# Pair sums of a mixture-of-experts layer, added by VectorE from PSUM instead of SBUF, with 24 buffers for the expert outputs instead of 16

## What is computed

```
x = x + attn(layernorm(x))
xf = layernorm(x)
weights, indices = top_k(softmax(xf @ Wg), 4)
y[token] += swiglu(xf[token], W1[e], W2[e], W3[e]) * weight   # for each of a token's four experts
z = swiglu(xf, Ws1, Ws2, Ws3)                                 # silu(xf @ Ws1) * (xf @ Ws3) @ Ws2
out = x + y + z
```

## Time and profile before

| | us |
|---|---|
| median of 3 runs | 640.11 |
| lowest and highest | 639.14, 641.84 |
| time of the profiled execution | 639.03 |
| its span | 637.3 |
| last stage, from the first h matmul at 551.39 to the end | 85.9 |
| mean granted clock of TensorE | 0.973 |

### The profile page before, as it was taken

One profiled execution on the slowest core, in us unless ns is written; L12 is line 12 of the kernel. 1 busy time (PEld: TensorE's weight loads), 2 busy tenths in 40 slices (PEclk: granted clock), 3 DMA queues, 4 the chain that ended last, 5 costly groups with the idle time before them and its releaser, 6 DMA issues.

```text
span 637.3 us, 16757 instructions
## 1 busy us (share of the span) xinstructions
PE 581.1 (91%) x4081; PEld 420.9 (66%) x4081; DVE 365.5 (57%) x1420; ACT 393.3 (62%) x1306; POOL 375.0 (59%) x425
## 2 busy tenths in 40 slices
PE   4799999999999977699899999999999999997981
PEld 1466766666676654268668888888888888554551
DVE  4589999999999995433223233322333223248686
ACT  2589988989898973216656766676666766410100
POOL 4124778787788786605445555565665555497360
PEclk9999999999999997699999999999999999998995
DMA  8994444444444547957776655565565555397773
GB/s 275 303 291 167 175 169 179 178 161 169 187 161 169 200 185 231 348 173 226 235 224 190 184 181 184 181 186 182 182 182 185 187 180 181 113 412 251 228 264 132
DMA packets 70154, 130.53 MB, mean 205 GB/s; under 512 B 10288, under 2 KB 48560, under 8 KB 70064
## 3 DMA queue, kind: packets, MB, share of 16 engines
q1 hardware_dynamic: 52128, 83.32, 41.1%
q0 software_dynamic: 13824, 41.96, 17.8%
q10 hardware_dynamic: 4112, 4.19, 2.0%
HBM read 61.11 MB, written 68.32 MB: 203 GB/s over the span
## 4 chain that ended last, share of the span: by engine, by line
PE 65%; POOL 10%; issue 8%; DVE 8%; SPq 4%; ACT 3%; DMA 2%; DVEq 0%; ACTq 0%; POOLq 0%
PE pS L730 19%; PE pS L742 9%; PE pS L554 8%; POOL xs L369 6%; PE pQV L659 4%; PE pS L590 3%; POOL w L387 3%; PE pT L723 2%; PE pO L676 2%; PE pQV L723 2%; PE pQV L568 2%; PE pO L568 2%; PE pO L642 1%; DVE xall L994 1%; PE pT L631 1%
## 5 line engine op out<-in xcount | busy, mean ns | idle before, releaser
L398 POOL DMA_INDIRECT ys<-gsh,dst x160 | 152.9, 956 | 131.9 <-ACT gsh L531 130.0
L730 PE MATMUL pS<-w,after_a 128*128 x640 | 165.8, 382 | 0.2 <-ACT after_a L520 0.2
L369 POOL DMA_INDIRECT xs<-xg,posi x128 | 124.3, 971 | 49.6 <-issue 25.6
L730 PEld LDWEIGHTS pS<-w,after_a 128*128 128x128 f32 x640 | 109.1, 190 | 9.8 <-issue 0.6
L742 PE MATMUL pS<-w,after_a 128*128 x320 | 95.6, 381 | 0.0
L1008 DVE COPY after_a<-pO 128x128 f32<-128x128 f32 x80 | 23.3, 292 | 93.0 <-PE pO L737 92.0
L1008 DVE COPY after_a<-pT 128x128 f32<-128x128 f32 x80 | 23.3, 292 | 92.8 <-PE pT L737 91.4
L531 ACT ACTIVATE gsh<-pS,xg 128x256 f32<-128x256 f32 x160 | 75.9, 474 | 0.4 <-issue 0.4
L530 ACT CAST dst<-xg 128x1 int32 x160 | 30.6, 191 | 60.9 <-PE pS L742 60.9
L659 PE MATMUL pQV<-w 128*128 128x512 f32 x128 | 64.0, 624 | 0.5 <-ACT w L464 0.5
L554 PE MATMUL pS<-x2T_all,ws 128*128 128x512 f32 x128 | 62.1, 640 | 2.4 <-DVE gsh L978 1.4
(11 more groups left out here) (157 smaller groups left out, 1105.8 us busy)
## 6 DMA issues: line engine op xcount, KB each, us to landing
xg<-xs SPq DMA_DIRECT2D x160, 160.0 KB, 2.2
ys<-gsh SPq DMA_DIRECT2D x32, 512.0 KB
w<-ys SPq DMA_DIRECT2D x32, 512.0 KB, 6.2
xs<-padrow SPq DMA_DIRECT2D x33, 160.0 KB, 2.4
w<-in_L_ffn_W ACTq DMA_DIRECT2D x1, 4096.0 KB, 21.9
out<-xall SPq DMA_DIRECT2D x32, 128.0 KB, 1.8
xall<-in_L_attn_X SPq DMA_DIRECT2D x1, 3072.0 KB, 14.0
ys<-gsh,dst POOLq DMA_INDIRECT x160, 2.7
```

What stands on the lines that cost most here:

```text
L369: pool.indirect_dma_start(out=xs, out_offset=bass.IndirectOffsetOnAxis(ap=posi[:, a.r8, k:k + 1], axis=0), in_=xr[:, a.r8, :], in_offset=N ...
L398: pool.indirect_dma_start(out=ys, out_offset=bass.IndirectOffsetOnAxis(ap=dst[:, j % 8:j % 8 + 1], axis=0), in_=y[:, j % 8, :], in_offset= ...
L730: last = pe.matmul(pS[a.b][:, 0:2 * F], xgT[:, a.b, k, :], w13[:, bass.ds(e, 1), k, :, :].rearrange("p a n f -> p (a n f)"), start=(k == 0 ...
```

## The change

- *The adds.* Behind GpSimd's sum, ScalarE copies both 128x256 sums of a tile from SBUF to a PSUM bank, `pT0` or `pT1` in turn (`copy_parts`, L552 of the new kernel). VectorE adds first the one half of the bank to `xall`, then the other (`add_parts`, L1060 and L1062), the second waiting for the first by `half_sum`. So there are two adds a tile as before, but each has one input in SBUF and one in PSUM. ScalarE fills a bank again when the tile two earlier is added (`added`).
- *The buffers.* `PB` is 24; the eight more lie where the expert weights `w2` were (`arena`).
- *SP.* It issues 24 loads, then the other 8, each when `parts_copied` says that ScalarE has copied the tile 24 earlier, and only then the 32 stores, each when its tile is complete.
- *Which addition comes last.* Up to tile 15 (`LATE` = 4 groups) z is added first and the parts last; from tile 16 on the parts come first and z last.
- *The order.* On VectorE and ScalarE it is written out step by step. TensorE's order is unchanged; its wait for z adds is split over two semaphores.

```diff
-    PB = 16
+    PB = 24
...
+        def parts(t):
+            b = t % PB
+            return parts_a[:, b] if b < 16 else parts_b[:, b - 16]
...
-            for t in range(NT + PB):
-                if t >= PB:
-                    sp.wait_ge(S["summed"], t - PB + 1)
-                    sp.dma_start(out_tiles[t - PB], xall[:, t - PB, :]).then_inc(final[t % 2], 16)
-                if t < NT:
-                    sp.dma_start(parts[:, t % PB, :, :], ys_tiles[t]).then_inc(parts_in[t % PB], 16)
+            for t in range(PB):
+                sp.dma_start(parts(t), ys_tiles[t]).then_inc(parts_in[t], 16)
+            for t in range(PB, NT):
+                sp.wait_ge(S["parts_copied"], t - PB + 1)
+                sp.dma_start(parts(t), ys_tiles[t]).then_inc(parts_in[t - PB], 16)
+            for t in range(NT):
+                if t < QT * LATE:
+                    sp.wait_ge(S["added"], t + 1)
+                else:
+                    sp.wait_ge(S["summed"], t - QT * LATE + 1)
+                sp.dma_start(out_tiles[t], xall[:, t, :]).then_inc(final[t % 2], 16)
...
-            for g in range(NPRE, NG):
-                shared_silu(g)
-
+            def copy_parts(t):
+                wait(act, S["parts_sum"], t + 1)
+                wait(act, S["added"], t - 1)
+                act.copy((pT0, pT1)[t % 2][:], parts(t)[:, 0:2, :].rearrange("p k c -> p (k c)")
+                         ).then_inc(S["parts_copied"], 1)
+
+            half_silu(2, 0)
+            half_silu(2, 1)
+            copy_parts(0)
...
-                    wait(pe, S["z_done"], QT * g + q - 1)
+                    wait(pe, S["z_done"], min(QT * g + q - 1, QT * LATE))
+                    wait(pe, S["summed"], QT * (g - LATE) + q - 1)
...
-                for t in range(g * QT, (g + 1) * QT):
-                    wait(dve, S["parts_sum"], t + 1)
-                    dve.tensor_tensor(parts[:, t % PB, 0, :], parts[:, t % PB, 0, :], parts[:, t % PB, 1, :], ALU.add
-                                      ).then_inc(S["half_sum"], 1)
-                for t in range(g * QT, (g + 1) * QT):
+            def add_parts(t):
+                wait(dve, S["parts_copied"], t + 1)
+                if t < QT * LATE:
                     wait(dve, S["z_done"], t + 1)
-                    wait(dve, S["half_sum"], t + 1)
-                    dve.tensor_tensor(xall[:, t, :], xall[:, t, :], parts[:, t % PB, 0, :], ALU.add).then_inc(S["summed"], 1)
+                dve.tensor_tensor(xall[:, t, :], xall[:, t, :], (pT0, pT1)[t % 2][:, 0:D], ALU.add).then_inc(S["half_sum"], 1)
+                wait(dve, S["half_sum"], t + 1)
+                dve.tensor_tensor(xall[:, t, :], xall[:, t, :], (pT0, pT1)[t % 2][:, D:2 * D], ALU.add).then_inc(S["added"], 1)
```

More of the change, by code:

```diff
@@ L533, in _ @@
             pipelined(NJ, 3, expert_step)
-            for g in range(NPRE, NG):
-                shared_silu(g)
+            def copy_parts(t):
[6 more added lines that the diff above has]
+            copy_parts(0)
+            copy_parts(1)
+            half_silu(3, 0)
+            copy_parts(2)
+            copy_parts(3)
+            half_silu(3, 1)
+            copy_parts(4)
+            copy_parts(5)
+            copy_parts(6)
+            copy_parts(7)
+            copy_parts(8)
+            half_silu(4, 0)
+            copy_parts(9)
+            copy_parts(10)
+            copy_parts(11)
+            half_silu(4, 1)
+            copy_parts(12)
+            copy_parts(13)
+            copy_parts(14)
+            copy_parts(15)
+            copy_parts(16)
+            half_silu(5, 0)
+            copy_parts(17)
+            copy_parts(18)
+            half_silu(5, 1)
+            copy_parts(19)
+            copy_parts(20)
+            copy_parts(21)
+            copy_parts(22)
+            copy_parts(23)
+            half_silu(6, 0)
+            copy_parts(24)
+            copy_parts(25)
+            copy_parts(26)
+            half_silu(6, 1)
+            copy_parts(27)
+            copy_parts(28)
+            copy_parts(29)
+            copy_parts(30)
+            copy_parts(31)
+            half_silu(7, 0)
+            half_silu(7, 1)
         @block.tensor
@@ L978, in shared_gate, with add_z @@
-                    dve.tensor_tensor(gsh[:, g % 2, m, :], sg[:, m, :], pS[2 * m + 1][:], ALU.mult).then_inc(S["gsh_done"], 1)
+                    half_gate(g, m)
+            def add_z(t):
+                wait(dve, S["z_ps"], t + 1)
+                if t >= QT * LATE:
+                    dve.wait_ge(S["added"], t + 1)
+                dve.tensor_tensor(xall[:, t, :], xall[:, t, :], (pQV, pO)[t % 2][:, 0:D], ALU.add
+                                  ).then_inc(S["z_done" if t < QT * LATE else "summed"], 1)
@@ L980, in shared_add @@
             def shared_add(g):
                 for q in range(QT):
[L982 to L991 removed]
+                    add_z(g * QT + q)
@@ L1016, in _ @@
                 dve.wait_ge(y_out[b], 16 * NJ // 8)
-            shared_gate(NPRE)
-            for g in range(NG):
-                if NPRE + 1 + g < NG:
-                    shared_gate(NPRE + 1 + g)
-                if NPRE + g < NG:
-                    shared_add(NPRE + g)
-                parts_add(g)
+            half_gate(2, 0)
+            half_gate(2, 1)
+            add_parts(0)
+            add_parts(1)
+            half_gate(3, 0)
+            add_parts(2)
+            add_parts(3)
+            half_gate(3, 1)
+            add_parts(4)
+            add_z(8)
+            add_z(9)
+            add_parts(5)
+            add_z(10)
+            add_z(11)
+            add_parts(6)
+            add_parts(7)
+            add_parts(8)
+            half_gate(4, 0)
+            add_parts(9)
+            add_parts(10)
+            add_parts(11)
+            half_gate(4, 1)
+            add_z(12)
+            add_z(13)
+            add_parts(12)
+            add_z(14)
+            add_z(15)
+            add_parts(13)
+            add_parts(14)
+            add_parts(15)
+            add_parts(16)
+            half_gate(5, 0)
+            add_parts(17)
+            add_parts(18)
+            half_gate(5, 1)
+            add_parts(19)
+            add_z(16)
+            add_z(17)
+            add_parts(20)
+            add_z(18)
+            add_z(19)
+            add_parts(21)
+            add_parts(22)
+            add_parts(23)
+            half_gate(6, 0)
+            add_parts(24)
+            add_parts(25)
+            add_parts(26)
+            half_gate(6, 1)
+            add_parts(27)
+            add_z(20)
+            add_z(21)
+            add_parts(28)
+            add_z(22)
+            add_z(23)
+            add_parts(29)
+            add_parts(30)
+            add_parts(31)
+            half_gate(7, 0)
+            half_gate(7, 1)
+            add_z(24)
+            add_z(25)
+            add_z(26)
+            add_z(27)
+            add_z(28)
+            add_z(29)
+            add_z(30)
+            add_z(31)
 _INS = ["L0_attn_X", "L0_attn_Wq", "L0_attn_Wv", "L0_attn_q_norm_w", "L0_attn_v_norm_w", "L0_ffn_Wg", "L0_ffn_W1",
```

26 lines of the change are left out of this document (14 added, 12 removed).

## The result

| | before | after |
|---|---|---|
| median, us | 639.71 (4 runs, 639.14 to 641.84) | 622.31 (4 runs, 620.32 to 623.50) |
| ratio | | 0.972, 95% interval 0.9686 to 0.9754 |
| profiled execution: time, span | 639.03, 637.3 | 622.96, 621.2 |
| last stage, first h matmul to the end | 637.3 - 551.39 = 85.9 | 621.2 - 552.42 = 68.8 |
| mean granted clock | 0.973 | 0.986 |

The forecast was 623.3 in a range of 620.5 to 628.5. The kernel is 17.4 us faster by the medians, and the last stage is 17.1 us shorter by the profile (it began 1.03 us later in this execution, so the spans differ by 16.1).

A forecast was written before the change was run, and what follows sets the result against it. It took the last stage as bound by 64 VectorE adds, half held by GpSimd, ahead of z adds TensorE awaits. Undisturbed span 617.9 plus 2.6 of waits is 620.5, a gain of 16.8 from 640.11: 623.3 us, range 620.5 to 628.5.

The forecast's parts named there:

- the three waits: TensorE in z(2), z(4), z(5): a pair of adds ahead of the first z add delays it 0.87 us, 2.6 together.
- the hold: Last stage: VectorE adds with both inputs in SBUF each wait out one GpSimd sum, taking 1.2 to 1.4 us.
- three of about 1.3: TensorE in z(2), z(4), z(5): idle times of about 1.3 us each, counting the 0.41 us already there.
- GpSimd's starvation: GpSimd's sums: loads ahead of all stores would feed its 32 sums without a break, the last done at 599.2.
- The term of 0.58 us a store: SP's queue: each store costs 0.58 us, so 24 stores are gone by 611 and all 32, if ready, by 615.6.
- The tail: End of the kernel: the last store costs 2.68 us between VectorE's last add and the span's end, and stays.
- A: Rival: stores behind the last load set the end, at 0.77 us each; 625 us, chance 12%.
- B: Rival: TensorE's clock falls at its three waits of 1.3 us, costing 5.1 us; 628.4 us, chance 6%.
- C: Rival: VectorE's adds from PSUM wait for GpSimd as well, so no gain; 640 us, chance 3%.
- D: Rival: tiles come too slowly, delaying the end from 1.59 us a tile on; 643 us, chance 4%.
- E: Rival: TensorE's three waits for VectorE in z(2), z(4), z(5) don't come; 620.7 us, chance 8%.
- The page's price of PSUM operands: VectorE's 64 adds: the skill page charges 0.065 us more each from PSUM, 4.1 us of VectorE time together.

The follow-up runs named there:

- e4: Kernel after, with VectorE's pair of part adds moved behind the first two z adds in groups 2, 4 and 5; 619.78 us, 0.967 of before.
- e12: Kernel after, but VectorE adds from SBUF without ScalarE's copies and GpSimd sums only 8 of 256 columns of each half; 0.974 of before.
- e11: Kernel before plus only ScalarE's copies and the adds from PSUM; 16 buffers, old SP and VectorE order; 0.986 of before.
- e1: Kernel before with only 24 buffers and all loads ahead of all stores on SP; 640.75 us, 0.999 of before.
- e3: Kernel after with 16 buffers instead of 24; 622.27 us, 0.970 of before.
- e10: Kernel after with 16 buffers and SP's old sequence, each store followed by the load of the tile 16 later; 0.975 of before.
- e6: Kernel after with a second ScalarE copy of the same size, into unused SBUF, ahead of each copy to PSUM; 626.65 us, 0.978 of before.
- e7: Kernel after with the second add of each tile taken from SBUF instead of PSUM; 0.981 of before.
- e2: Kernel after without ScalarE's copies, VectorE adding both halves straight from SBUF; 642.06 us, 1.002 of before.

## Why the prediction was right

*The sum.* Each term beside what it measured:

| term | forecast | measured |
|---|---|---|
| TensorE from h(2) to its end, with three waits | 614.81 - 551.39 + 2.6 = 66.0 | 66.15 |
| the three waits, in z(2), z(4), z(5) | 3 x 0.87 = 2.6 | 0.80 + 0.89 + 0.89 = 2.58; gone in e4, worth 2.4 |
| pair of adds, start to start | 0.80 (0.46 + 0.34) | 0.79 (567.69 to 568.48) |
| ScalarE's copy | 0.65 (0.59 to 0.95) | 0.59 |
| last z add | 0.42 | 0.45 |
| end of VectorE to the end of the span | 2.68 | 2.2 |
| stage | 69.1 | 68.8 |

The step that carried it was to build TensorE's undisturbed schedule from the chain's 10.60 us periods and to add the waits that the new order leaves. It asked of VectorE only that it be early enough, and with 42.3 us of work in the 72 us from 550 to 622 it was.

*The size of the waits.* That 2.58 was measured where 2.6 was said is in part luck. The sum let the pair wait for ScalarE's copy, 0.67 us behind the gate's start. It starts 0.60 behind it (567.09 to 567.69), and 0.61 in e12, where there is no copy: at its 0.59 us the copy is in time, and the pair costs 0.79, not 0.87. What filled the sum up is the 0.1 us of z(4) and z(5) that stays in e4. And "three of about 1.3" did not come: the 0.41 us from which it was counted is idle time of the weight loads, while the matmuls stood still for 0.17 there (566.09 to 567.13, where 0.87 is the usual step). Theirs became 0.80 to 0.89.

*What bounds the stage.* The prediction read the hold out of the earlier trace rows and named it as the bound. e12 shows the hold to be what it was taken for. But "that is what bounds the last stage" was too simple: with the hold gone and the order as before (e11), the stage is 9.8 us longer than after. The sum was right all the same, since it took the tail of parts behind the last z add as gone, which only the new order makes it. The prediction should have named the two gains apart, 8.6 us on TensorE and 8.0 behind it. Whoever had read it as "the PSUM adds are worth 17 us" would have been wrong by 10.

*The buffers and SP's order.* "This takes GpSimd's starvation away" is true and worth nothing (e1, e3, e10). "24 loads go at once" is not true: SP needs 19.3 us for them. The consequences that were drawn held nevertheless. The last sum ends at 601.5; 599.2 was said for a stage that began 1.03 earlier, so it is 1.3 later, by 1.2 us of short waits for DMA. The stores ready by then were gone at 608, with 611 forecast, as a window of the kernel after shows, the first with the DMA idle (0.06; it was 0.82 in the 2 us before):

```profile
608.00:610.00 2.00, 2.00 (x6) 0.89 (x5) 0.69 (x1) 0.52 (x1) 0.00 (x0) 1.00 0.06 18
```

The term of 0.58 us a store was too dear: SP's queue had 75.9% of 72 us, 54.6 us, which less 32 loads at 1.25 is 0.46 each.

*The tail.* It was 2.68 and is 2.2, because the last tiles now end 0.86 apart and SP has nothing else to issue: the last store is issued at 619.1, right behind the add that ends at 619.02; before, with adds 0.335 apart, it was issued at 635.0, 0.4 behind the add that ended at 634.62. This and e11's tail of 692.2 - 690.0 = 2.2 agree.

*The rivals.* A (stores set the end): no, the DMA is idle between 608 and the stores of the last tiles. B (the clock falls): no, each 2 us window from 554 to 620 has a granted clock of 1.00. But the waits were 0.8 to 0.9 us and not the 1.3 that B assumed; at 1.33 and 1.42 (e6, e7) the matmuls kept their pace too, and behind some longer waits they did not, see below. C (PSUM adds are held too): no, as the single lines of the kernel after show, that of the copy first (durations ns least/median/most):

```profile
L552 ACT COPY pT<-w x32: 587/590/592, 560.7 to 605.8; 128x512 f32<-128x512 f32 x32
```

```profile
L1060 DVE TENSOR_TENSOR xall<-xall,pT x32: 412/416/422, 561.4 to 606.4; 128x256 f32<-128x256 f32 x32
```

D (slow tiles): no, but e10 comes near its threshold of 1.59, with 1.49 us a tile. E (no waits): no, but e4 shows what it is worth: 2.5 us against the median of e3, 2.4 by the traces, where 2.6 was said.

*The page's price of PSUM operands.* The Trainium skill (VectorE: DVE Perf Modes, the section on the TRN2 errata) would have made each add 0.065 us dearer than one from SBUF, an estimate from its cycle counts. e12 has the comparison that was missing, the same add from an SBUF that nobody holds: 0.418 us (L1057) against 0.416 from PSUM (L1060), and 0.424 against 0.421 for the second add of a pair. The rows decide: in this kernel they cost the same.

## What to carry to other kernels

An engine that is slowed by a neighbour (here VectorE's adds with both inputs in SBUF beside GpSimd's) costs twice: what waits for it, and the work that is then still left behind the last step. Removing the slowdown gives the first only; the second needs an order that uses the freed time, and that order alone can make things worse while the slowdown is there, so both have to be tried together. Before buffers are added to feed an engine, look whether anyone waits for it, and whether the issuing queue could fill them; and in front of an add that TensorE waits for, put nothing that can stand behind it.

## What the runs showed of the hardware that was not expected

- SP's issue of DMAs gets slower while many are in flight: 24 loads of 512 KB took 19.3 us to issue, where 16 took 8.94 in the kernel before; single issues took up to 2.98 us, and the later loads landed 15.7 to 17.1 us after their issue. So a load can wait at SP although its buffer is free.
- The hold costs both sides: GpSimd's sums take 1.38 us each beside SBUF adds (e2) and 1.28 beside PSUM adds.
- TensorE's clock: behind waits of 1.33 and 1.42 us (e6, e7) the z tiles kept their 1.03 to 1.13 us; behind waits of 1.87 (e1), 1.98 (e6) and 2.65 us (e7) some ran slower, 1.52 to 1.91 us a tile, and the ten us from there on have a granted clock of 0.83 in each (597 to 607, 604 to 614, 650 to 660). But behind waits of 1.80 (e1) and 2.28 us (e11), both in z(7) with two tiles left to do, the tiles took 1.13 and 1.03. So the length of the wait alone does not decide; what does was not tried.
- A load of 512 KB and a store of 128 KB in turn come every 1.57 us (e10, but for one gap); the load alone takes 1.25, and the store by the queue's time in the kernel after 0.46.
- ScalarE copies 128x512 from SBUF to PSUM in 0.590 us and from SBUF to SBUF in 0.614.
